# Selective-scan kernel: the last state of each group gets its input from another PSUM bank, and VectorE's passes stand in other steps

## The chip, the cores and the metric

The kernel runs on one core of one Trainium2 chip. The metric is the device time of one execution in microseconds (us), as the median of several runs; smaller is better. The kernel before takes 1560.38 us (three runs, 1560.03 to 1560.77).

## The reference, cut to what matters

x has 8 sequences of 1024 tokens with 256 features, float32. A Mamba layer with a residual is followed by a feed-forward layer with a residual; both begin with a layer norm.

```python
xz = x @ in_proj_w.T                 # 256 -> 2 x 512: xp and z
xc = silu(causal_conv4(xp))
dt, B, C = split(xc @ x_proj_w.T)    # 64, 16, 16
delta = softplus(dt @ dt_proj_w.T + dt_proj_b)
h[t] = exp(delta[t] * A) * h[t-1] + delta[t] * B[t] * xc[t]     # 512 channels x 16 states
y[t] = sum over states of h[t] * C[t] + D * xc[t]
x = x + (y * silu(z)) @ out_proj_w.T
x = x + shared_ffn(layernorm(x)) + routed_ffn(...)
```

The routed experts' weights are truncated to whole numbers; they are almost always zero, and then that part is skipped.

## The kernel before

Work goes by chunks of 512 tokens: 16 chunks c, two to a sequence (HV = 2). Channels lie on the partitions, in 4 groups g of 128. A chunk has S = 32 steps s, eight to a group; a step handles Q = 2 of the 16 states of its group over all 512 tokens. k = 32c + s counts steps. Each engine has its queue written out by hand, step by step (`tensor`, L446; `scalar`, L805; `vector`, L1116; `gpsimd`, L1326; `sync`); semaphores tie them together. TensorE's queue runs two steps behind VectorE's for the sums.

In a step:
- ScalarE writes da = exp(delta * A) for step k + 5 (`act_exp`, L638).
- VectorE scans both states (`dve_scan`, L974): h = da * h + B*u, where B*u is read from BX, four PSUM banks that hold four states of one group. u is delta * xc.
- GpSimd multiplies hs by C (`pool_times_c`, L1271).
- TensorE adds the products of step k - 2 to Y by eight transposes (`pe_sum`, L263), and at the end of each odd step refills BX with B*u of the next four states (`pe_bx`, L239): for each of 4 token blocks and 4 row quarters one matmul of uT (u transposed) with bd, a matrix that holds B on block diagonals. There is one BX, so a refill waits until all four states in it are scanned (`e.wait_ge(s_scan, RT * m)`, L228), and the next scan waits for the refill.

Beside this run, spread over the steps, for neighbouring chunks: the input product and convolution (`pe_xp` L299, `act_xp` L673 and L675, three taps on VectorE, L1005 and L1009, in the bank of Y that is idle); delta (`pe_dt` L349, `act_softplus` L741 to L745, `dve_delta` L1044); u (`pool_u` L1289) and its transposes (`pe_ut` L357, `act_ut` L758); dbc and B transposed (L333, L723, L340, L730), from which SP's queue writes bd by DMA (`sp_bd`, L1406); the gate (L1066), transposed (`pe_yt`, L365; `act_yt`, L765); output product, second norm and shared layer (L376, L1072, L1028, L1035, L775, L386, L396, L1082, L404, L413, L1113). x of chunk c + 2 is transposed in two halves (`pe_trc` L273, `act_trc` L654). Banks PA and PB are shared by these in an order written in BANK_A and BANK_B (step: stage, chunk offset, index): each user waits until the one before it has released the bank. VectorE's passes stand behind the scans of odd steps. `pe_fill` (L444) and others put in matmuls with no use for the result in places where TensorE would stand idle.

## Time and profile before

| | |
|---|---|
| median of 3 runs | 1560.38 us |
| profiled execution, span | 1559.1 us |
| TensorE matmuls busy | 1454.6 us, 93% |
| TensorE weight loads busy | 1134.1 us, 73% |
| VectorE busy | 1475.8 us, 95% |
| ScalarE busy | 1257.4 us, 81% |
| GpSimd busy | 1399.0 us, 90% |
| granted TensorE clock, mean | 0.999 |

The span is the time from the first to the last instruction of the profiled execution; it is 1.3 us below the median of the runs. Engines are PE (TensorE matmuls), PEld (its weight loads), DVE (VectorE), ACT (ScalarE), POOL (GpSimd) and SP (SyncE). Lines are those of the kernel before. In a timeline, rows of like instructions are merged: start, length, engine, line, operation, output and input, count, and in brackets the idle time ahead of it and what ended that.

### The profile page before, as it was taken

The page shows a single profiled execution, that of the slowest core. Times are in us where ns is not written, and L with a number is a line of the kernel's source. Part 1 is how long each engine was busy: PE and PEld are TensorE (multiplying, and loading weights), DVE is VectorE, ACT ScalarE, POOL GpSimd, SP SyncE. Part 2 cuts the span into 40 slices and gives each one's busy share as a digit, 9 for nine tenths or more (in the row PEclk, how much of TensorE's full clock was granted, in tenths as well). Part 3 has the DMA queues.
Part 4 walks back from the last instruction along what each step waited for, and adds up shares of the span by engine and source line. Part 5 has one row for each costly group of instructions (what it writes and reads, how often), then busy time and mean ns, then how long its engine had stood idle before and what let it go on. Part 6 is the DMA issues. An engine that isn't in the chain of part 4 may idle for free.

```text
span 1559.1 us, 39641 instructions
## 1 busy us (share of the span) xinstructions
PE 1454.6 (93%) x15324; PEld 1134.1 (73%) x15324; DVE 1475.8 (95%) x1775; ACT 1257.4 (81%) x2099; POOL 1399.0 (90%) x1199
## 2 busy tenths in 40 slices
PE   8889999999999999999999999999999999999988
PEld 5666777776777777777777777767777677777777
DVE  6999999999999999999999999999999999998886
ACT  7987887887888888887887888888888887788752
POOL 2899999999999999998999989999998999989994
PEclk9999999999999999999999999999999999999999
DMA  5103031040402305032040301304031040401301
GB/s 161 61 3 136 2 101 66 9 157 3 143 22 65 101 3 164 1 93 73 4 163 3 138 28 47 120 3 164 2 97 69 4 149 3 137 15 43 123 2 56
DMA packets 78512, 106.48 MB, mean 68 GB/s; under 512 B 42289, under 2 KB 67761, under 8 KB 70130
## 3 DMA queue, kind: packets, MB, share of 16 engines
q1 hardware_dynamic: 78322, 103.92, 20.8%
q8 instruction: 123, 2.02, 0.5%
q14 instruction: 67, 0.55, 0.1%
HBM read 86.10 MB, written 17.30 MB: 66 GB/s over the span
## 4 chain that ended last, share of the span: by engine, by line
DVE 32%; PE 20%; ACT 18%; issue 17%; POOL 10%; DMA 1%; SPq 1%; DVEq 1%; ACTq 0%; POOLq 0%
DVE hs L974 29%; PE BX L239 9%; ACT da L638 8%; POOL hs L1271 8%; PE Y L299 3%; PE Y L263 2%; ACT xc L705 1%; DMA cb<-c_scratch 1%; SPq L1406 1%; ACT xp L673 1%; DVE st L986 1%; DVE Y L1005 1%; PE PB L349 1%; ACT x2n L775 1%; POOL rstd L1304 1%
## 5 line engine op out<-in xcount | busy, mean ns | idle before, releaser
L1271 POOL TENSOR_TENSOR hs<-hs,cb 128x1024 f32<-128x1024 f32 x512 | 1210.2, 2364 | 76.3 <-DVE hs L974 55.3
L974 DVE TENSOR_TENSOR_SCAN hs<-da,BX 128x512 f32<-128x512 f32 x1024 | 1165.6, 1201 | 55.5 <-PE BX L239 46.5
L638 ACT ACTIVATE da<-delta,a_neg 128x511 f32<-128x511 f32 (+1 forms) x1024 | 663.6, 711 | 24.9 <-DVE hs L974 24.5
L263 PEld LDWEIGHTS Y<-ident,hs 128*128 128x128 f32 x4096 | 464.5, 141 | 97.3 <-issue 58.0
L263 PE MATMUL Y<-ident,hs 128*128 128x128 f32 x4096 | 510.1, 273 | 14.5 <-POOL hs L1271 14.4
L239 PE MATMUL BX<-bd,uT 32*128 32x128 f32 x8192 | 301.3, 284 | 77.9 <-DVE hs L974 73.8
L239 PEld LDWEIGHTS BX<-bd,uT 32*128 32x128 f32 x8192 | 252.5, 187 | 138.8 <-DVE hs L974 137.7
L299 PE MATMUL Y<-xnT,w_in 128*128 128x512 f32 x240 | 117.6, 613 | 0.7 <-ACT gate L691 0.7
L673 ACT ACTIVATE xp<-Y 128x512 f32<-128x512 f32 x60 | 35.9, 598 | 100.4 <-PE Y L299 99.9
L324 PE MATMUL PA<-w_in,xnT 128*128 128x512 f32 x240 | 114.5, 599 | 0.0
L1005 DVE SCALAR_TENSOR_TENSOR Y<-xp,w_conv,Y 128x512 f32<-128x512 f32 x120 | 88.9, 741 | 3.0 <-ACT Y L675 1.4
L1289 POOL TENSOR_TENSOR u<-delta,xc 128x512 f32<-128x512 f32 x63 | 80.4, 1277 | 5.1 <-issue 5.1
L1267 POOL COPY hlast<-hs 128x2 f32<-128x2 f32 x256 | 47.7, 186 | 38.5 <-DVE hs L974 36.8
L324 PEld LDWEIGHTS PA<-w_in,xnT 128*128 128x128 f32 x240 | 43.2, 190 | 44.9 <-issue 43.1
L741 ACT ACTIVATE u<-PB 128x512 f32<-128x512 f32 x63 | 37.5, 596 | 46.8 <-PE PB L349 45.1
L349 PE MATMUL PB<-dbc,w_dt 97*128 97x512 f32 x126 | 70.9, 645 | 0.9 <-DVE dbc L1136 0.9
L758 ACT ACTIVATE uT<-PB 128x512 f32<-128x512 f32 x48 | 28.7, 597 | 49.8 <-PE PB L357 49.8
L299 PEld LDWEIGHTS Y<-xnT,w_in 128*128 128x128 f32 x240 | 40.8, 190 | 36.5 <-issue 28.7
L333 PE MATMUL PA<-xc,w_x 128*96 128x512 f32 x128 | 61.6, 603 | 0.2 <-ACT xc L687 0.2
L376 PE MATMUL PB<-w_out,ygT 128*128 128x256 f32 x240 | 60.8, 386 | 0.9
L376 PE MATMUL PA<-w_out,ygT 128*128 128x256 f32 x240 | 60.8, 386 | 0.0
L1281 POOL TENSOR_TENSOR da<-first,hlast 128x2 f32<-128x2 f32 x256 | 51.1, 199 | 0.0
(194 smaller groups left out, 1517.5 us busy)
## 6 DMA issues: line engine op xcount, KB each, us to landing
cb<-c_scratch SPq DMA_DIRECT2D x64, 1024.0 KB, 4.8
x<-in_x SPq DMA_DIRECT2D x16, 512.0 KB, 4.3
x_scratch<-x2T SPq DMA_DIRECT2D x16, 512.0 KB, 6.8
xt<-in_x SPq DMA_DIRECT2D x15, 512.0 KB, 5.3
bd<-bt SPq DMA_DIRECT2D x480, 1.0 KB
out<-x SPq DMA_DIRECT2D x15, 512.0 KB, 3.2
w_in<-in_in_wT SPq DMA_DIRECT2D x1, 1024.0 KB, 8.4
c_scratch<-dbc SPq DMA_DIRECT2D x64, 8.0 KB, 1.5
```

Of the source, the lines that this page charges most:

```text
L239: mm = e.matmul(BX[:, q * CH + j * P:q * CH + (j + 1) * P], uT[rows, g, j, :], bd[rows, (NR * c + p) % BR, j, :, :].rearrange("p t n -> p ...
L263: mm = e.matmul(Y[(G * c + g) % 2][:, t * P:(t + 1) * P], hs[:, k % HR, q, t * P:(t + 1) * P], ident[:, :], is_transpose=True, start=False ...
L299: mm = e.matmul(bank[:, :], w_in[:, kk, g * P:(g + 1) * P], xnT[c % 2][:, kk, :], start=(kk == 0), stop=(kk == KD - 1))
L324: mm = e.matmul(bank[:, :], xnT[c % 2][:, kk, t * P:(t + 1) * P], w_in[:, kk, ED:2 * ED], start=(kk == 0), stop=(kk == KD - 1))
L333: mm = e.matmul(PA[0:FX, :], w_x[:, g, :], xc[:, (G * c + g) % XR, :], start=(g == 0), stop=(g == G - 1))
L349: e.matmul(bank[:, :], w_dt[:, g * P:(g + 1) * P], dbc[:, :].rearrange("f (j q t) -> f q j t", j=J, q=RT), start=True, stop=True).then_inc ...
L376: mm = e.matmul(bank[:, t2 * DM:(t2 + 1) * DM], ygT[:, g, t * P:(t + 1) * P], w_out[:, g, :], start=(g == 0), stop=(g == G - 1))
L638: e.activation(da[:, k % DR, q, h:], delta[:, g, h:], ACT.Exp, scale=a_neg[:, g, n:n + 1]).then_inc(s_da, 1)
L974: e.tensor_tensor_scan(hs[:, k % HR, q, :], da[:, k % DR, q, :], BX[:, :].rearrange("p (t n) -> p n t", n=RT)[:, n % RT, :], float(c % HV) ...
L1005: e.scalar_tensor_tensor(out=bank[:, :], in0=xp[:, g, kk:kk + CH], scalar=w_conv[:, g, kk:kk + 1], in1=bank[:, :], op0=ALU.mult, op1=ALU.a ...
L1271: e.tensor_tensor(hs[:, k % HR, :, :], hs[:, k % HR, :, :], cb[:, Q * p:Q * p + Q, :], ALU.mult).then_inc(s_hc, 1)
L1289: e.tensor_tensor(u[:, m % UR, :].rearrange("p (j q t) -> p q j t", j=J, q=RT), delta[:, g, :].rearrange("p (q j t) -> p q j t", j=J, q=RT ...
```

## The change

State 15 of each group is no longer computed into BX. ScalarE multiplies uT by B's column of state 15 (`act_v`, four instructions, in steps 5, 13, 20 and 29), and TensorE transposes the result (`pe_bu`, four transposes, in steps 7, 15, 23 and 31) into a bank of its own: the bank of Y that is idle for groups 0, 1 and 3, PA for group 2. The second scan of a group's last step reads that bank. The refill behind such a step waits for 15 states of the group instead of 16, and the refill of the last four states of a group writes three of them. B transposed (`bt`) has two buffers. VectorE's scans of a step are separate calls, with passes between and behind them in other steps than before; two of the other users of PA and PB move to Y[0] (the first half of the shared product, z of block 1), and delta and u of group 1, uT of group 1, the transposes of the gate and of x stand in other steps. Fill matmuls go from steps 7 and 23 to 25. `prob` shares its memory with `is_top`. Of the schedule of VectorE the new lines are shown; renamed variables are left out.

```diff
-          12: [("trc0", 2, 0)], 16: [("z", 1, 1)], 18: [("dbc", 1, 0)], 22: [("bt", 1, 0)],
+          12: [("trc0", 2, 0)], 18: [("dbc", 1, 0)], 22: [("bt", 1, 0)], 23: [("bu", 0, 2)],
           24: [("otr", -1, 0)], 25: [("otr", -1, 1)], 27: [("hl", -1, 1)], 30: [("z", 1, 2)]}
...
+BANK_B = {2: [("yt", -1, 2), ("trc", 2, 0)], 3: [("trc", 2, 1)], 4: [("ut", 0, 1)], 6: [("dt", 0, 2)],
+          8: [("res", -1, 0)], 13: [("trc0", 2, 1)], 16: [("dt", 0, 3)], 18: [("yt", 0, 0)], 20: [("ut", 0, 3)],
+          21: [("yt", 0, 1)], 24: [("dt", 1, 0)], 26: [("hl", -1, 0)], 28: [("ut", 1, 0)], 29: [("ht", -1, 0)],
+          30: [("dt", 1, 1), ("yt9", 0, 2)]}
...
-        bt = sb("bt", [P, NR, J, RT])
+        bt = [sb(f"bt{i}", [P, NR, J, RT]) for i in range(2)]
+        v = sb("v", [P, J, P])
...
-        prob = sb("prob", [P, NQ, TB, NE])
+        prob = is_top
...
+            if (stage, i) == ("o", 0):
+                return Y[0], c, s_o0, s_o0_out
+            if (stage, i) == ("z", 1):
+                return Y[0], c - 1, s_z1, s_z1_out
+            if stage == "bu" and i != 2:
+                return Y[(i + 1) % 2], 3 * c + min(i, 2), s_bu, s_bu_out
...
+        def scanned(k):
+
+            c, i = divmod(k, S)
+            g, p = divmod(i, NP)
+            return released("bu", c, g) if p == NP - 1 else (s_scan, (N - 1) * (G * c + g) + Q * (p + 1))
+
...
         def pe_bx(e, m):
             c, i = divmod(m, QC)
             g, p = divmod(i, NR)
-            e.wait_ge(s_scan, RT * m)
+            e.wait_ge(s_scan, (N - 1) * (m // NR) + RT * p)
...
+            ns = RT - 1 if p == NR - 1 else RT
             for j in range(J):
                 for q in range(RT):
                     rows = slice(q * KT, (q + 1) * KT)
-                    mm = e.matmul(BX[:, q * CH + j * P:q * CH + (j + 1) * P], uT[rows, g, j, :],
-                                  bd[rows, (NR * c + p) % BR, j, :, :].rearrange("p t n -> p (t n)"), start=True,
+                    mm = e.matmul(BX[:, q * CH + j * P:q * CH + (j + 1) * P].rearrange("p (t n) -> p t n", n=RT)[:, :, 0:ns],
+                                  uT[rows, g, j, :], bd[rows, (NR * c + p) % BR, j, :, 0:ns], start=True,
                                   stop=True, tile_position=(q * KT, 0))
             mm.then_inc(s_bx, 1)
+
+        def pe_bu(e, c, g):
+            bank, n, done, out = bank_of("bu", c, g)
+            e.wait_ge(out, n)
+            if g != 2:
+                e.wait_ge(s_gm, G * c + g)
+            conv = {0: 5 if c == 0 else G * c + 6, 1: G * c + 7, 3: G * c + 9}.get(g, 0)
+            if conv and on(c + 1 if g < 2 else c + 2):
+                e.wait_ge(s_yx_out, conv - G + 1)
+            e.wait_ge(s_v, G * c + g + 1)
+            for j in range(J):
+                mm = e.transpose(bank[:, :].rearrange("p (q j t) -> p j q t", q=RT, j=J)[:, j, :, :], v[:, j, :], ident[:, :])
+            mm.then_inc(done, 1)
         def pe_skip(e, c, g):
             m = G * c + g
             e.wait_ge(s_gm, max(0, m - 1))
+            if m:
+                e.wait_ge(*released("bu", *divmod(m - 1, G)))
+            if g == 2 and on(c + 1):
+                e.wait_ge(*released("z", c + 1, 1))
+            if g == 0 and on(c - 2):
+                e.wait_ge(*released("o", c - 2, 0))
...
+            if v == G + 2:
+                e.wait_ge(*released("bu", 0, 0))
...
         def pe_z(e, c, t):
             bank, n, done, out = bank_of("z", c, t)
             e.wait_ge(out, n)
+            if t == 1:
+                e.wait_ge(*released("bu", c - 1, 1))
...
         def pe_shared(e, c, kk):
             bank, n, done, out = bank_of("o", c, kk)
             e.wait_ge(out, n)
+            if kk == 0:
+                e.wait_ge(*released("bu", c + 1, G - 1))
...
+            e.wait_ge(*released("bu", *divmod(m - 1, G)))
...
-                    if s == 2:
+                    if s == 4:
...
-                    if s == 2 and c and on(c + 2):
-                        pe_trc(e, c + 2, 0)
                     if s in (12, 13) and c == 0:
                         pe_trc(e, 2, s - 12)
                     if on(c - 1):
+                        if s == 2:
+                            pe_yt(e, c - 1, 2)
                         if s == 4:
-                            pe_yt(e, c - 1, 2)
...
+                    if s % NP == NP - 1:
+                        pe_bu(e, c, s // NP)
...
-                    if s == 3 and c and on(c + 2):
-                        pe_trc(e, c + 2, 1)
-                    if s == 15:
+                    if s in (2, 3) and c and on(c + 2):
+                        pe_trc(e, c + 2, s - 2)
+                    if s == 18:
...
-                    if c == NQ - 2 and s in (23, 29):
+                    if c == NQ - 2 and s in (25, 29):
                         pe_fill(e, c, s, 5)
-                    if c == NQ - 1 and s in (5, 7, 13, 17, 21, 23, 29):
+                    if c == NQ - 1 and s in (5, 13, 17, 21, 25, 29):
...
+            e.wait_ge(*released("bu", NQ - 1, G - 1))
...
         def act_exp(e, k, parts=range(2)):
             c, i = divmod(k, S)
             g, p = divmod(i, NP)
-            e.wait_ge(s_scan, max(0, Q * (k - DR + 1)))
+            if k >= DR:
+                e.wait_ge(*scanned(k - DR))
...
 +        def act_v(e, c, g):
+            m = G * c + g
+            e.wait_ge(*released("ut", c, g))
+            if c:
+                e.wait_ge(*released("bt", c, 0))
+            else:
+                e.wait_ge(s_b15, 1)
+            if m:
+                e.wait_ge(*written("bu", *divmod(m - 1, G)))
+            for j in range(J):
+                ins = e.activation(v[:, j, :], uT[:, g, j, :], ACT.Copy, scale=bt[c % 2][:, NR - 1, j, RT - 1:RT])
+            ins.then_inc(s_v, 1)
...
         def act_bt(e, c):
             bank, n, done, out = bank_of("bt", c, 0)
             e.wait_ge(done, n + 1)
-            e.wait_ge(s_bdd, 16 * KT * (c - 1))
-            e.activation(bt[:, :, :, :], bank[:, 0:J * FX].rearrange("p (j f) -> p j f", j=J)[:, :, R:R + N].rearrange(
+            e.wait_ge(s_bdd, 16 * KT * max(0, c - 2))
+            e.activation(bt[c % 2][:, :, :, :], bank[:, 0:J * FX].rearrange("p (j f) -> p j f", j=J)[:, :, R:R + N].rearrange(
                 "p j (r n) -> p r j n", r=NR), ACT.Copy).then_inc(out, 1)
 ...
-                    if s == 2:
-                        act_ut(e, c, 1)
+                    if s == 2 and on(c - 1):
+                        act_yt(e, c - 1, 2)
                     if s in (3, 4) and c and on(c + 2):
                         act_trc(e, c + 2, s - 3)
                     if s == 4 and c and on(c + 1):
                         act_xp(e, G * c + 6)
                     if s == 4 and on(c - 1):
-                        act_yt(e, c - 1, 2)
                         act_yt(e, c - 1, 3)
+                    if s == 4:
+                        act_ut(e, c, 1)
...
-                    if s == 8:
-                        act_silu_z(e, c)
+                    if s in (5, 13, 20, 29):
+                        act_v(e, c, s // NP)
                     if s in (12, 13) and c == 0:
                         act_trc(e, 2, s - 12)
                     if s == 7:
                         if on(c + 1):
                             act_z(e, c + 1, 0)
                         act_skip(e, c, 1)
+                    if s == 8:
+                        act_silu_z(e, c)
                     if s == 5 and c == 0:
                         act_norm(e, 2)
                     if s == 15:
                         act_skip(e, c, 2)
+                    if s == 18:
...
-        def dve_scan(e, k):
+        def dve_scan(e, k, q):
             c, i = divmod(k, S)
             g, p = divmod(i, NP)
-            e.wait_ge(s_bx, k // 2 + 1)
-            e.wait_ge(s_y, max(0, k - HR + 1))
-            if c % HV:
-                e.wait_ge(s_cr, S * (c // HV) + i + 1)
-            for q in range(Q):
-                n = Q * p + q
-                e.wait_ge(s_da, Q * k + q + 1)
+            if q == 0:
+                e.wait_ge(s_bx, k // 2 + 1)
+                e.wait_ge(s_y, max(0, k - HR + 1))
+                if c % HV:
+                    e.wait_ge(s_cr, S * (c // HV) + i + 1)
+            n = Q * p + q
+            e.wait_ge(s_da, Q * k + q + 1)
+            if n == N - 1:
+                bank, use, done, out = bank_of("bu", c, g)
+                e.wait_ge(done, use + 1)
+                e.tensor_tensor_scan(hs[:, k % HR, q, :], da[:, k % DR, q, :], bank[:, :],
+                                     float(c % HV), ALU.mult, ALU.add).then_inc(out, 1)
+            else:
...
         def dve_bd(e, p):
             if p == 0:
                 e.wait_ge(*written("bt", 0, 0))
+            if p == NR - 1:
+                e.tensor_copy(bt[0][:, NR - 1, :, RT - 1], PA[:, 0:J * FX].rearrange("p (j f) -> p j f", j=J)[
+                    :, :, R + N - 1]).then_inc(s_b15, 1)
...
+                e.wait_ge(s_b15, 1)
...
+                    dve_scan(e, k, 0)
+                    if s == 14 and on(c + 1):
+                        dve_tap(e, G * c + 7 if c else G + 3, 1)
+                    if s == 24 and on(c + 2):
+                        dve_tap(e, G * c + 8, 0)
+                    dve_scan(e, k, 1)
+                    if s == 1:
+                        if c == 0:
+                            dve_tap(e, G, 0)
+                            dve_tap(e, G, 1)
+                        else:
+                            if on(c - 2):
+                                dve_shared(e, c - 2, 0)
+                            dve_delta(e, c, 1)
+                    if s == 3:
+                        if c == 0:
+                            dve_tap(e, G, 2)
+                        if on(c - 2):
+                            dve_shared(e, c - 2, 1)
+                        if on(c - 1):
+                            dve_gate(e, c - 1, 3)
+                    if s == 5 and on(c + 1):
+                        dve_tap(e, G * c + 6 if c else G + 1, 0)
+                        dve_tap(e, G * c + 6 if c else G + 1, 1)
+                    if s == 6 and on(c + 1):
+                        dve_tap(e, G * c + 6 if c else G + 1, 2)
                     if s == 7:
                         dve_delta(e, c, 2)
+                    if s == 9:
+                        if c == 0:
+                            for kk in range(K - 1):
+                                dve_tap(e, G + 2, kk)
+                        elif on(c + 3):
                             dve_stats(e, c + 3, 0)
                             dve_stats(e, c + 3, 1)
+                    if s == 11:
+                        dve_gate(e, c, 0)
+                        if on(c - 1):
+                            dve_residual(e, c - 1, 0)
+                    if s == 13:
+                        if on(c + 1):
+                            dve_tap(e, G * c + 7 if c else G + 3, 0)
+                        if on(c - 1):
+                            dve_stats2(e, c - 1, 0)
+                    if s == 14 and on(c + 1):
+                        dve_tap(e, G * c + 7 if c else G + 3, 2)
+                    if s == 17:
+                        if on(c - 1):
+                            dve_residual(e, c - 1, 1)
+                        dve_delta(e, c, 3)
+                    if s == 19:
+                        dve_gate(e, c, 1)
+                        if on(c - 1):
+                            dve_stats2(e, c - 1, 1)
+                    if s == 21:
+                        if on(c - 1):
+                            dve_aggr2(e, c - 1)
+                        if on(c + 3):
                             dve_aggr(e, c + 3)
+                    if s == 24 and on(c + 2):
+                        dve_tap(e, G * c + 8, 1)
+                    if s == 25:
+                        if on(c + 2):
+                            dve_tap(e, G * c + 8, 2)
+                        if on(c + 1):
                             dve_delta(e, c + 1, 0)
+                    if s == 27:
+                        dve_gate(e, c, 2)
+                        if on(c - 1):
+                            dve_top(e, c - 1, 0)
+                    if s == 28 and on(c - 1):
+                        dve_top(e, c - 1, 1)
+                    if s == 29 and on(c + 2):
+                        dve_tap(e, G * c + 9, 0)
+                        dve_tap(e, G * c + 9, 1)
+                    if s == 30 and on(c + 2):
+                        dve_tap(e, G * c + 9, 2)
...
         def pool_times_c(e, k):
             c, i = divmod(k, S)
             g, p = divmod(i, NP)
-            e.wait_ge(s_scan, Q * (k + 1))
+            e.wait_ge(*scanned(k))
...
-            e.wait_ge(s_scan, Q * (k - DR + 1))
+            e.wait_ge(*scanned(k - DR))
...
+                        if s == 1 and c:
+                            pool_u(e, c, 1)
                         if s == 7:
                             pool_u(e, c, 2)
                         if s == 17:
                             pool_u(e, c, 3)
-                    if on(c + 1):
-                        if s == 25:
-                            pool_u(e, c + 1, 0)
-                        if s == 31:
-                            pool_u(e, c + 1, 1)
+                    if s == 25 and on(c + 1):
+                        pool_u(e, c + 1, 0)
...
-                            bt[t:P:KT, :, :, :]).then_inc(s_bdd, 16)
+                            bt[c % 2][t:P:KT, :, :, :]).then_inc(s_bdd, 16)
```

## Rows read from the trace of the kernel before

**Rows 1.** The page: busy us, share of the span, instructions of each engine
```profile
PE 1454.6 (93%) x15324; PEld 1134.1 (73%) x15324; DVE 1475.8 (95%) x1775; ACT 1257.4 (81%) x2099; POOL 1399.0 (90%) x1199
```

**Rows 2.** Windows: us; busy (count) of PE, PEld, DVE, ACT, POOL; granted clock; DMA share; GB/s
```profile
694.00:788.00 94.00, 89.20 (x946) 69.35 (x945) 91.79 (x111) 78.87 (x134) 87.31 (x71) 1.00 0.23 71
...
1501.30:1504.70 3.40, 3.40 (x40) 3.17 (x41) 2.55 (x5) 0.47 (x1) 2.95 (x4) 0.50 0.00 0
```

**Rows 3.** Waits of VectorE: total us, times, longest us
```profile
DVE hs L974 <- PE BX L239: 46.5, 76, 1.3
```

**Rows 4.** Timeline of VectorE in chunk 7 (its step 5 ends at 709.8)
```profile
709.78 1.52 DVE L1005 SCALAR_TENSOR_TENSOR Y<-xp,w_conv,Y 128x512 f32<-128x512 f32 x2
711.21 4.55 DVE L974 TENSOR_TENSOR_SCAN hs<-da,BX 128x512 f32<-128x512 f32 x4
715.68 0.72 DVE L1009 SCALAR_TENSOR_TENSOR xc<-xp,w_conv,Y 128x512 f32<-128x512 f32 x1
716.32 0.68 DVE L1044 SCALAR_TENSOR_TENSOR delta<-PB,u 128x512 f32<-128x512 f32 x1
717.06 4.55 DVE L974 TENSOR_TENSOR_SCAN hs<-da,BX 128x512 f32<-128x512 f32 x4
...
745.55 0.74 DVE L1028 BATCH_NORM_STATS2 st<-x 128x6 f32<-128x256 f32 x2
...
758.04 4.56 DVE L974 TENSOR_TENSOR_SCAN hs<-da,BX 128x512 f32<-128x512 f32 x4 [0.76 <-PE BX L239]
...
774.84 0.24 DVE L1082 MAX8 top<-PB 128x8 f32<-128x8 f32 x2
775.11 0.17 DVE L1084 TENSOR_TENSOR is_top<-PB,top 128x16 f32<-128x16 f32 x1
```

**Rows 5.** Timeline of TensorE's matmuls in chunk 7 (steps 2, 5 to 7, 21 to 23)
```profile
700.39 1.03 PE L413 MATMUL PA<-w_s,x2n 128*128 128x256 f32 x4
701.25 0.60 PE L273 MATMUL PB<-ident,xt 128*128 128x128 f32 x4
...
709.92 1.17 PE L239 MATMUL BX<-bd,uT 32*128 32x128 f32 x32
711.02 1.12 PE L349 MATMUL PB<-dbc,w_dt 97*128 97x512 f32 x2
711.99 1.04 PE L263 MATMUL Y<-ident,hs 128*128 128x128 f32 x8
712.86 1.88 PE L324 MATMUL PA<-w_in,xnT 128*128 128x512 f32 x4
...
715.81 0.39 PE L239 MATMUL BX<-bd,uT 32*128 32x128 f32 x4 [0.20 <-DVE hs L974]
...
757.91 1.99 PE L299 MATMUL Y<-xnT,w_in 128*128 128x512 f32 x4
759.73 0.49 PE L340 MATMUL PA<-ident,dbc 96*128 96x96 f32 x4
760.06 1.91 PE L263 MATMUL Y<-ident,hs 128*128 128x128 f32 x16
762.65 0.39 PE L239 MATMUL BX<-bd,uT 32*128 32x128 f32 x4 [0.68 <-DVE hs L974]
```

**Rows 6.** Groups by shape: count, busy us, mean ns of one, idle before
```profile
L752 ACT ACTIVATE xc<-xc,d_skip 128x512 f32<-128x512 f32 x64 | 45.4, 710 | 0.0
L730 ACT ACTIVATE bt<-PA 128x64 f32<-128x64 f32 x15 | 3.3, 223 | 16.2 <-PE PA L340 16.2
```

**Rows 7.** Timeline of ScalarE in chunk 7, steps 2 and 3
```profile
700.64 1.32 ACT L638 ACTIVATE da<-delta,a_neg 128x511 f32<-128x511 f32 x2
701.89 0.60 ACT L654 ACTIVATE xnT<-PB 128x512 f32<-128x512 f32 x1
```

**Rows 8.** Timeline of VectorE behind the last scan
```profile
1537.87 2.31 DVE L1093 SCALAR_TENSOR_TENSOR prob<-den,is_top 128x480 f32<-128x480 f32 x1 [0.29 <-ACT den L792]
```

**Rows 9.** Timeline of TensorE in chunk 15
```profile
1501.16 1.14 PE L239 MATMUL BX<-bd,uT 32*128 32x128 f32 x16 [2.06 <-DVE hs L974]
```

83 lines of the change are left out of this document (11 added, 72 removed).

## The prediction

> **What bounds the kernel now.** I read the page's busy times first: VectorE 95%, TensorE's matmuls 93%, GpSimd 90% [rows 1]. No engine has much air, so the question is which order of events repeats. The windows show a chunk of 94 us at the full granted clock, with TensorE busy for 89.2 us of it and VectorE for 91.8 us [rows 2]. VectorE waits for the refill of BX 76 times, 46.5 us in all [rows 3]; those are only the waits that a profile can see.
>
> The timeline of VectorE shows the rhythm [rows 4]. Four scans take 4.55 us: each is 1.20 us long and the next starts 1.11 us after it. Then BX, of which there is one copy, has to be refilled. The scans that began at 711.21 end at 715.76; at 715.81 the refill starts on TensorE and takes 1.17 us [rows 5], and the next scan starts at 717.06: 1.30 us from the last scan's end, though the passes between (715.68, 716.32) are done before. Two taps in a gap run 1.52 us and stretch it by 0.05 us (709.78 to 711.21). From the start of one refill to the next it is therefore 5.85 us, in three of sixteen cases 5.90. A chunk is 13 x 5.85 + 3 x 5.90 = 93.75 us, and sixteen chunks make 1500 of the 1559.1 us. The kernel is bound by "four scans, then a refill"; passes in the gap cost nothing up to 1.3 us.
>
> The timeline of TensorE shows how late the next refill could be without anybody noticing [rows 5]. Consecutive groups overlap by 0.16 us, so a group costs its length less 0.16; behind BX, 1.10; and a refill that follows without idle time costs 0.09 more. Steps 6 and 7 hold 1.10 + 0.97 + 0.87 + 1.72 + 0.87 + 0.09 = 5.62 us against 5.89 granted: only 0.2 to 0.3 us of air. VectorE's floor and TensorE's floor lie that close in many pairs of steps.
>
> **The change, part by part.** I time refill starts, naming each by the step behind which it comes (R5 to R7 and so on).
>
> *State 15 leaves BX.* The refill behind steps 7, 15, 23 and 31 may start after the third scan, and the fourth, 1.11 us, lies in the gap. That takes 4 x 1.11 = 4.4 us a chunk off VectorE's path if the refill really starts then.
>
> *Passes leave the gaps.* Six taps and one pair of top-8 passes now run between scans that no refill separates. A tap costs 0.64 us there (715.68 to 716.32 [rows 4]), the top-8 passes about 0.40 (two maxima and the comparison, 774.84 to 775.11 and 0.17 less overlap). In a gap they cost nothing before; now they cost 6 x 0.64 + 0.40 = 4.2 us a chunk. This alone eats what state 15 saved.
>
> *The refill of a group's last four states writes three of four columns.* It was 1.17 us for 32 matmul records of 128 columns. The row with 96 columns (four transposes of dbc, 0.49 us against 0.60 for 128 columns [rows 5]) says that time goes with columns: bounds 0.96 (all scales) and 1.17 (nothing does). I take 0.97, 0.20 less, as the nearest row scales.
> The Trainium skill (TensorE: Matmul & The Clock Gate, section "Wait — 56ns, not 53.3ns?") speaks against that: starts of matmuls are never closer than about 25 ns. BX's are 29 ns apart here; by the rule the refill would shrink by 0.12 us only, and the sum below would be some 4 us higher. No row shows it.
>
> *TensorE's four transposes (bu)* cost 0.60 - 0.16 = 0.44 us, and stand in its queue ahead of a sum (0.87) and of the refill. In steps 7, 15 and 31 they wait for the last tap of the convolution that uses the same bank, and everything behind them waits too.
>
> *ScalarE's four scalings* of 128 columns: the nearest rows are 0.22 us (64 columns) and 0.71 (512 columns) [rows 6]; four cost 0.9 to 2.8, I take 1.3. ScalarE is busy for 78.9 of 94 us [rows 2] and writes da about five steps ahead, so they lie in idle time. The upper bound would delay delta in step 7 by some 0.3 us (low bound: nothing).
>
> *GpSimd and SP's queue* keep their work; u of group 1 moves from step 31 to step 1 and is ready before its transposes in step 4. The copies for bd read a second buffer and are issued no later. B is scaled out of its own copy. The copy added before the first chunk lies where VectorE has 0.5 us idle. Merging prob with is_top costs nothing.
>
> Now the sixteen intervals of an inner chunk. VectorE's path: refill 1.24 to the first scan (1.04 with three columns), 1.11 a scan, 1.20 for the last, 0.05 to the next refill.
> - R5 to R7: VectorE 1.29 + 2.22 + 0.64 + 1.20 + 0.05 = 5.40; TensorE 0.90 (1.10 less 0.20) + 0.97 + 0.87 + 1.72 + bu 0.44 + 0.87 + 0.09 = 5.87. TensorE decides: -0.03 against 5.90. R29 to R31 has the same instructions: +0.02.
> - R13 to R15: scans and taps reach the end of the last tap 4.76 us after R13: a tap and two statistics (745.55 [rows 4]) fill 1.18, then 1.11 + 0.64 + 1.11 + 0.72; then bu, sum and refill: + 0.05 + 0.44 + 0.87 + 0.09 = 6.22. +0.32.
> - R21 to R23: VectorE could at 4.51. TensorE 0.90 + 1.82 + 0.33 + 1.75 + 0.44 + 0.09 = 5.33 [rows 5]: -0.52.
> - R23 to R25: two taps between the scans: 1.24 + 3 x 1.11 + 1.28 + 1.20 + 0.05 = 7.10: +1.20.
> - R27 to R29: the second top-8 passes: +0.40.
> - R1 to R3: both transposes of x now have one sum between them instead of two. The second needs ScalarE's copy of the first out of the same bank, and that stands behind yT's copy and two exps (1.32 [rows 7]). Refill, skip, shared product and yT's transposes end 3.06 us after R1 (1.10 + 0.49 + 0.87 + 0.60 [rows 5]); then 0.53 + 1.22 + 0.60 on ScalarE, and 0.6 us of transposes: refill 0.16 us late. The second copy holds uT's bank: 0.04 more in R3 to R5.
> - The other eight stay at 5.85. In the gaps of steps 21, 23, 27 and 31 VectorE idles as before or more (0.76 us at 758.04 was there already [rows 4]).
>
> Sum: -0.03 + 0.02 + 0.32 - 0.52 + 1.20 + 0.40 + 0.16 + 0.04 = +1.6 us a chunk, 13 inner chunks: +20.7. Chunk 0, with less on TensorE, about +0.8; chunk 14 +0.8; the last has no taps and little on TensorE, two of its groups save about 1 us each and the top-8 passes cost 0.4: -1.4. Tail: the product that goes into Y[0] waits for the last scan, and the 2.31 us pass at 1537.87 [rows 8] with it: +0.8. Total +21.7 on an execution with a span of 1559.1, 1.3 under the median of 1560.4: **1582 us**.
>
> **Rivals.**
> *TensorE keeps up (faster).* If refill and transposes were always ready when VectorE comes, R5 to R7 is 5.40 but R7 to R9 6.15 (state 15 and delta fill 1.6 us), R13 to R15 5.93, R21 to R23 4.51, R29 to R31 5.40, R1 to R5 unchanged: 93.4 us a chunk, with the ends 1555 us. For it: BX has 0.2 to 0.7 us of air before most refills (0.68 at step 23). Against it: the air is smaller than what bu and the earlier start ask, by 0.8 us in step 23. It decides where a pair's matmuls take less than VectorE's 4.5 to 5.4 us.
> *They cancel:* half of TensorE's lateness, no wait for the tap: about 1560.
> *The short refill is no shorter and the scalings are dear:* R5 to R7, R21 to R23 and R29 to R31 each 0.2 longer, 0.15 for delta: some 10 us, 1592.
> *The clock falls.* In the last chunk TensorE once stood idle for 2.06 us [rows 9] and a stretch of 3.4 us at 0.50 of the clock (1.2 GHz) followed [rows 2], which made that interval 0.8 us longer. R23 to R25 now has about 2.4 us of idle time on TensorE in two pieces; if the clock fell there in each chunk: +11 us, 1594. Elsewhere idle pieces of 1 us left the clock at 1.00, so I think it unlikely.
>
> **How the numbers follow.** A measurement of this kernel tells about 0.2%, 3 us, from no change. The forecast, about +1% to +2%, gets 0.62; refill not shorter or the clock 0.18; cancelling 0.07; TensorE keeps up 0.13. Faster 0.13, same 0.07, slower 0.80. The range goes from the faster rival, 1555, to a little over the dear cases, 1600; the slower cases alone fill 1566 to 1600.
>
> **What would show it.** In the changed profile: the refill behind step 23 starts some 0.8 us after its third scan instead of 0.05; between R23 and R25 7.1 us; a wait of VectorE for BX behind state 15 in steps 15, 23 and 31 (0.3 to 0.9 us) and still 0.6 in step 21; a refill record of about 0.97 us behind steps 5, 13, 21, 29; chunks of 95.4 us. Chunks under 93.7 us would refute the argument, above all if TensorE's refill starts on time behind state 14.

## The result, and the profile after

The changed kernel takes 1614.16 us (median of four runs, 1612.09 to 1615.67), the kernel before in the same session 1560.3 us (1560.03 to 1560.77). The ratio is 1.0343, with an interval of 1.0328 to 1.0357: 3.4% slower. The forecast was 1582 us in a range of 1555 to 1600; the direction was right and the size less than half of what came. All times below are medians of runs like these; one run of all, of "State 15 back in BX", took 2091.56 us at a mean granted clock of 0.65, and it is left out.

The page's busy times of the kernel after:

```profile
PE 1487.4 (92%) x15568; PEld 1162.1 (72%) x15568; DVE 1479.0 (92%) x1776; ACT 1328.7 (82%) x2355; POOL 1403.0 (87%) x1199
```

Beside [rows 1], VectorE has 3 us more work and 55 us more of span: its loss is waiting. ScalarE has 71 us more, which is a first hint. The chain of waits shows it by pairs (who waits, for whom, us, how often, mean us), in the kernel after:

```profile
DVE hs L1043 <- PE BX L256: 89.8, 122, 2.8
PEld PA L416 <- ACT uT L817: 15.1, 15, 1.2
PE Y L271 <- DVE xc L1078: 19.4, 15, 2.9
```

VectorE's waits for BX have nearly doubled against [rows 3] (46.5 us, 76 times). The other two are new, and each comes about once a chunk: TensorE waits for ScalarE's copy of uT, and the new transposes (L271) wait for the last tap. To place them I took the start of the first scan behind each refill from the trace. Mean of chunks 1 to 13, us, "R5 to R7" being the stretch from the refill behind step 5 to the one behind step 7 (differences are taken before rounding):

| stretch | before | forecast difference | after | difference |
|---|---|---|---|---|
| R1 to R3 | 5.85 | +0.16 | 6.08 | +0.23 |
| R5 to R7 | 5.84 | -0.03 | 6.00 | +0.16 |
| **R9 to R11** | 5.85 | **0** | 6.70 | **+0.85** |
| R11 to R15 | 11.74 | +0.32 | 12.38 | +0.64 |
| R19 to R25 | 17.67 | +0.68 | 18.52 | +0.85 |
| R25 to R29 | 11.70 | +0.40 | 12.26 | +0.56 |
| R29 to R31 | 5.85 | +0.02 | 5.98 | +0.13 |
| the other five | 29.30 | +0.04 | 29.31 | +0.01 |
| chunk | 93.80 | +1.6 | 97.24 | +3.44 |

The prediction timed the starts of the refills themselves. By these, R5 to R7 is 6.04, R13 to R15 6.54, R21 to R23 5.51 and R29 to R31 6.03 us, where 5.87, 6.22, 5.33 and 5.87 were forecast; the chunk is the same.

13 x 3.44 = 44.7 us. Chunk 0 costs 3.50 more, chunk 14 2.94, the last 1.45 less; the start is 0.77 and the tail 4.24 longer. The sum, 54.7, is the difference of the spans (1613.8 less 1559.1). Half of the chunk's extra is in two places, and one of them was not forecast at all.

**R9 to R11, where nothing was forecast.** TensorE's timeline in steps 10 and 11 of chunk 7, after (start, length, engine, line, operation, count, idle time ahead and what ended it):

```profile
747.81 0.60 PE L397 MATMUL PA<-ident,u 128*128 128x128 f32 x4
749.11 1.04 PE L299 MATMUL Y<-ident,hs 128*128 128x128 f32 x8
751.07 1.13 PE L416 MATMUL PA<-w_out,ygT 128*128 128x256 f32 x4 [0.92 <-ACT uT L817]
```

The transposes of u are written into PA at 747.81 and the output product wants PA at 750.15; it gets it at 751.07, when ScalarE has copied uT out. ScalarE's timeline over the same time, after:

```profile
736.82 1.27 ACT L764 ACTIVATE v<-uT,bt 128x128 f32<-128x128 f32 x4
...
744.68 1.28 ACT L773 ACT_TABLE_LOAD   x1
745.97 1.91 ACT L773 ACTIVATE gate<-gate 128x2048 f32<-128x2048 f32 x1
747.90 1.28 ACT L774 ACT_TABLE_LOAD   x1
749.20 1.33 ACT L684 ACTIVATE da<-delta,a_neg 128x511 f32<-128x511 f32 x2
750.44 0.57 ACT L817 ACTIVATE uT<-PA 128x512 f32<-128x512 f32 x1
```

The copy (750.44) is the last of a row without a gap: the gate's SiLU, between two table loads of 1.28 us, then two exps. The four scalings at 736.82 have pushed this whole row back by their length.

**R21 to R25, where most was forecast.** TensorE's timeline in steps 22 and 23 of chunk 7, after, and VectorE's in steps 22 to 24:

```profile
786.16 1.04 PE L299 MATMUL Y<-ident,hs 128*128 128x128 f32 x8
787.04 0.60 PE L271 MATMUL PA<-ident,v 128*128 128x128 f32 x4
787.48 1.04 PE L299 MATMUL Y<-ident,hs 128*128 128x128 f32 x8
788.44 1.17 PE L256 MATMUL BX<-bd,uT 32*128 32x128 f32 x32
```

```profile
785.28 2.31 DVE L1043 TENSOR_TENSOR_SCAN hs<-da,BX 128x512 f32<-128x512 f32 x2
787.75 1.22 DVE L1040 TENSOR_TENSOR_SCAN hs<-da,PA 128x512 f32<-128x512 f32 x1 [0.15 <-PE PA L271]
789.68 1.22 DVE L1043 TENSOR_TENSOR_SCAN hs<-da,BX 128x512 f32<-128x512 f32 x1 [0.72 <-PE BX L256]
790.82 0.73 DVE L1074 SCALAR_TENSOR_TENSOR Y<-xp,w_conv,Y 128x512 f32<-128x512 f32 x1
791.46 1.21 DVE L1043 TENSOR_TENSOR_SCAN hs<-da,BX 128x512 f32<-128x512 f32 x1
792.59 0.73 DVE L1074 SCALAR_TENSOR_TENSOR Y<-xp,w_conv,Y 128x512 f32<-128x512 f32 x1
```

BX is free at 787.59, TensorE is without any idle time and comes to the refill at 788.44, 0.85 us later (0.8 in the prediction). Scan and TensorE's transposes lie beside each other as meant, but VectorE then waits 0.72 us, and in the next pair the two taps between scans are on its path for their whole length. R23 to R25 is 7.17 us (7.10 forecast).

**R13 to R15.** TensorE's timeline, after:

```profile
758.85 1.15 PE L256 MATMUL BX<-bd,uT 32*128 32x96 f32 x32 [0.15 <-DVE hs L1043]
...
761.76 1.04 PE L299 MATMUL Y<-ident,hs 128*128 128x128 f32 x8
763.95 0.63 PE L271 MATMUL Y<-ident,v 128*128 128x128 f32 x4 [1.16 <-DVE xc L1078]
764.42 1.04 PE L299 MATMUL Y<-ident,hs 128*128 128x128 f32 x8
```

A refill of three states takes 1.15 us, one of four 1.17: it is hardly shorter. And the bank of Y is free only behind the third tap of the convolution (it ends at 763.69), 0.26 us before the transposes start; sum and refill stand behind them in TensorE's queue.

**The ends.** In chunk 0 and in the tail TensorE stands idle and then runs at half the clock. Its rows at the starts of the two stretches, and the windows of those (busy us of PE, PEld, DVE, ACT and POOL, granted clock, DMA share, GB/s), after:

```profile
82.93 1.08 PE L271 MATMUL Y<-ident,v 128*128 128x128 f32 x4 [2.93 <-DVE xc L1078]
1587.65 1.73 PE L463 MATMUL Y<-w_s,x2n 128*128 128x256 f32 x4 [2.00 <-DVE hs L1040]
```

```profile
82.90:86.20 3.30, 3.27 (x23) 2.97 (x27) 2.12 (x2) 1.23 (x3) 2.53 (x3) 0.51 0.00 0
1588.00:1591.40 3.40, 3.40 (x10) 2.69 (x9) 1.91 (x3) 0.30 (x2) 2.16 (x1) 0.50 0.02 5
```

At 82.93 four transposes take 1.08 us instead of 0.60. The granted clock is 0.5 (1.2 GHz) in both; R13 to R15 of chunk 0 alone is 2.2 us longer. The wait and the lower clock can be told apart in the tail. The runs with four columns and with the scalings in step 3 (below) have the same queue there and the same wait of 2.00 us, but the clock stays at 1.00, and from the first scan behind the last refill to the end they take 29.18 and 29.19 us. The kernel after and three other runs with this queue, all at the lower clock, take 30.87 to 30.89. Of the 4.24 us the clock is therefore 1.7. The run with four columns:

```profile
1589.02 1.10 PE L463 MATMUL Y<-w_s,x2n 128*128 128x256 f32 x4 [2.00 <-DVE hs L1040]
```

**Chunk 13.** The clock fell in one inner chunk too, behind a wait of 1.88 us for the refill of step 25. In chunk 11 TensorE has as much idle time between R23 and R25, 2.08 us, but in two pieces of 0.84 and 1.24 us. TensorE's row in chunk 13, and the window behind it, after:

```profile
1378.66 1.17 PE L256 MATMUL BX<-bd,uT 32*128 32x128 f32 x32 [1.88 <-DVE hs L1043]
```

```profile
1379.80:1383.20 3.40, 3.40 (x20) 3.40 (x17) 3.35 (x4) 1.39 (x4) 3.40 (x4) 0.50 0.08 9
```

R25 to R27 of that chunk is 6.94 us for 5.85. This one place is the whole +0.08 of R25 to R27 in the mean.

### The profile page after: what moved, and what is told of

It reads as the page before. It is cut to its first block, busy times and chain, and to the rows that moved or that the text cites. A ratio compares the mean times of both kernels' runs of the same rounds, so it can differ in the third digit from the quotient of the medians.

```text
span 1613.8 us, 40703 instructions
## 1 busy us (share of the span) xinstructions
PE 1487.4 (92%) x15568; PEld 1162.1 (72%) x15568; DVE 1479.0 (92%) x1776; ACT 1328.7 (82%) x2355; POOL 1403.0 (87%) x1199
## 4 chain that ended last, share of the span: by engine, by line
PE 29%; DVE 26%; issue 19%; ACT 17%; POOL 5%; DMA 2%; SPq 1%; DVEq 1%; ACTq 0%; POOLq 0%
DVE hs L1043 22%; PE BX L256 12%; ACT da L684 7%; PE Y L299 5%; POOL hs L1354 4%; PE Y L337 3%; DVE Y L1074 3%; PE PA L364 1%; ACT v L764 1%; SPq L1488 1%; ACT L774 1%; ACT L773 1%; DMA cb<-c_scratch 1%; PE PA L416 1%; PE Y L271 1%
## 5 line engine op out<-in xcount | busy, mean ns | idle before, releaser
L1043 DVE TENSOR_TENSOR_SCAN hs<-da,BX 128x512 f32<-128x512 f32 x960 | 1105.1, 1203 | 97.0 <-PE BX L256 89.8
L299 PE MATMUL Y<-ident,hs 128*128 128x128 f32 x4096 | 523.5, 273 | 17.2 <-POOL hs L1354 16.3
L364 PE MATMUL PA<-w_in,xnT 128*128 128x512 f32 x180 | 86.2, 601 | 0.0
L764 ACT ACTIVATE v<-uT,bt 128x128 f32<-128x128 f32 x256 | 81.2, 392 | 0.0
L1040 DVE TENSOR_TENSOR_SCAN hs<-da,Y 128x512 f32<-128x512 f32 x48 | 58.2, 1212 | 1.3 <-ACT da L684 0.7
L824 ACT ACTIVATE ygT<-PB 128x512 f32<-128x512 f32 x48 | 28.1, 586 | 34.8 <-PE PB L405 34.8
```

Source lines behind the costliest of these rows:

```text
L299: mm = e.matmul(Y[(G * c + g) % 2][:, t * P:(t + 1) * P], hs[:, k % HR, q, t * P:(t + 1) * P], ident[:, :], is_transpose=True, start=False ...
L364: mm = e.matmul(bank[:, :], xnT[c % 2][:, kk, t * P:(t + 1) * P], w_in[:, kk, ED:2 * ED], start=(kk == 0), stop=(kk == KD - 1))
L764: ins = e.activation(v[:, j, :], uT[:, g, j, :], ACT.Copy, scale=bt[c % 2][:, NR - 1, j, RT - 1:RT])
L1043: e.tensor_tensor_scan(hs[:, k % HR, q, :], da[:, k % DR, q, :], BX[:, :].rearrange("p (t n) -> p n t", n=RT)[:, n % RT, :], float(c % HV) ...
```

## The experiments

Each starts from the changed kernel and differs by the edit shown, with the last three excepted: they build on one another, from the run with all repairs on. Of the run with state 15 back in BX and of the one with all repairs the main lines are shown. A difference is counted against the changed kernel, the ratio against the kernel before on the same chip (medians 1560.3 to 1560.9 us).

**State 15 back in BX, the passes left where the change put them.** It removes the scalings, the transposes and the early refill.

```diff
-            return released("bu", c, g) if p == NP - 1 else (s_scan, (N - 1) * (G * c + g) + Q * (p + 1))
+            return s_scan, Q * (k + 1)
...
-            e.wait_ge(s_scan, (N - 1) * (m // NR) + RT * p)
+            e.wait_ge(s_scan, RT * m)
...
-                        pe_bu(e, c, s // NP)
...
-                        act_v(e, c, s // NP)
```

> State 15 is computed into BX and scanned from there as before the change; ScalarE's scalings and TensorE's transposes for it are left out; everything else of the change, above all where VectorE's passes stand, is kept. This is the price of the new places of the passes alone. Theory A: passes between scans cost their full length: R5 to R7 6.49, R13 to R15 7.13, R23 to R25 7.13, R27 to R29 6.25, R29 to R31 6.54 us, the rest 5.85 and 5.90: 98.0 us a chunk against 93.8, so about 1560 + 15 x 4.2 = 1620 to 1625, a little above the changed kernel: the idle bank then saves under 1 us a chunk of the 4.4 it takes out of the scans. Rival B: the passes cost little and the transposes and scalings are what made it slow: between 1560 and 1590.

1641.28 us (median of three runs), 1.0520 (1.0499 to 1.0542), 16 us above the upper end of what was expected. R9 to R11 has lost its extra (5.85 us). The chunk is 5.25 us longer than before, but that mean is of two kinds of chunk: 98.28 us (98.0 were expected from the passes alone), and 99.75 in every second one, where the clock falls. TensorE's row in chunk 7, the window behind it, and the same row one chunk later, in this kernel:

```profile
777.67 1.93 PE L256 MATMUL BX<-bd,uT 32*128 32x128 f32 x32 [2.32 <-DVE hs L1036]
```

```profile
777.00:782.00 5.00, 4.33 (x36) 2.85 (x37) 2.97 (x4) 0.44 (x1) 2.84 (x4) 0.66 0.00 0
```

```profile
877.42 1.17 PE L256 MATMUL BX<-bd,uT 32*128 32x128 f32 x32 [2.32 <-DVE hs L1036]
```

The wait is 2.32 us in both, in steps 14 and 15; behind the first TensorE is at the lower level and its refill takes 1.93 us, behind the second it is not. So theory A holds: a pass between scans costs its length. And the idle bank is worth something: with it the mean chunk is 1.8 us shorter than with these passes alone, some 1.0 of it at the full clock and 0.8 because the clock falls less often. It has to pay for the passes, 4.5 us at the full clock, and does not.

**Refill with all four columns.**

```diff
-            ns = RT - 1 if p == NR - 1 else RT
+            ns = RT
```

> The refill of a group's last four states writes all four columns again (128 columns a matmul instead of 96). Theory A: with 96 columns it takes as long as with 128 (1.15 to 1.17 us in the changed kernel's profile), because something other than the columns sets the pace, so nothing changes: 1614, within 3 us. Rival B, the one in my prediction: 0.20 us are saved somewhere in each of four refills, three of which decide; then the time rises by 14 x 0.6 = 8 us.

1614.82 us, 1.0343 (1.0326 to 1.0360): no difference beyond the noise. The 0.20 us that the prediction took off each three-column refill are 0.03 in the trace (1.15 us for 1.17).

**Refill with one column**, to see whether columns matter at all. States 13 and 14 are then not refilled.

```diff
-            ns = RT - 1 if p == NR - 1 else RT
+            ns = 1 if p == NR - 1 else RT
```

> The refill of a group's last four states writes one of four columns (32 a matmul); states 13 and 14 are scanned from what was in the bank. It asks what sets the refill's 1.17 us. Theory A: something that does not go with the columns (the 32 weight loads, or a smallest distance between matmuls): 1.1 to 1.17 us again, matmuls 28 to 29 ns apart. Rival B: a smallest distance of about 25 ns: 0.78 + 0.27 = 1.05 us. Rival C: columns: 0.5 us. The time changes by under 3 us in A.

One run: 1614.27 us. The refill takes 1.10 us with 32 columns instead of 1.15 with 96. Its beginning, cut off behind the first 4 and behind the first 16 of the 32 records, in the kernel after (96 columns) and then in this one (32):

```profile
734.33 0.36 PE L256 MATMUL BX<-bd,uT 32*128 32x96 f32 x4
734.33 0.70 PE L256 MATMUL BX<-bd,uT 32*128 32x96 f32 x16
```

```profile
733.70 0.32 PE L256 MATMUL BX<-bd,uT 32*128 32x32 f32 x4
733.70 0.65 PE L256 MATMUL BX<-bd,uT 32*128 32x32 f32 x16
```

The first four differ by 0.04 us; the next twelve add 0.34 and 0.33 us. By the single starts in the trace the records come in eight packs of four: the four of a pack start 7 ns apart, and from the second pack on a pack starts 112 ns behind the one before, with 128, 96 and 32 columns alike. Only the first distance goes with the columns (213, 187 and 133 ns). So theory A has the size (1.10 us, and the time did not change), but its 28 to 29 ns, as rival B's 25, would be a mean of 7 and 92 (26.5 here): what costs is one of eight packs. What sets the 112 ns is not shown; the weight loads of the packs start 108 to 112 ns apart as well, and no run changed them. The chunk follows the refill: 97.31 us with four columns, 97.24 with three, 97.10 with one.

**The scalings in step 3.**

```diff
-                    if s in (5, 13, 20, 29):
+                    if s in (3, 13, 20, 29):
                         act_v(e, c, s // NP)
```

> One part of the changed kernel is moved: ScalarE's four scalings for group 0 stand in step 3, where ScalarE waits 2.5 us for the convolution's input anyway, instead of step 5. Theory A: the interval of steps 10 and 11 is 6.70 us instead of 5.85 because the scalings (1.27 us) push the SiLU of z with its two table loads, and behind it the copy of uT of group 2, 1 us back, and TensorE's output product waits for that copy to leave bank PA. Then this interval falls back to 5.85 to 5.95 us and the time falls by 14 x 0.8 = 11 to 12 us, to about 1602. Rival B: the interval is long because TensorE has too much to do in it; then nothing changes (1614, within 3 us).

1613.16 us, 1.0336 (1.0319 to 1.0354), where 1602 was expected. R9 to R11 is back at 5.85 us: the scalings were the cause. But R3 to R5 grew by 0.84, and the time stayed. TensorE there, in this kernel:

```profile
728.94 1.17 PE L256 MATMUL BX<-bd,uT 32*128 32x128 f32 x32
...
731.35 0.66 PE L397 MATMUL PB<-ident,u 128*128 128x128 f32 x4 [1.24 <-ACT xnT L700]
```

Now the copy of xnT out of PB is late, and the transposes of u wait for it. The miss moved to the next user of a bank.

**The scalings in step 4**, ahead of the input product's copy.

```diff
+                    if s == 4:
+                        act_v(e, c, 0)
...
-                    if s in (5, 13, 20, 29):
+                    if s in (13, 20, 29):
```

> As the run with the scalings of group 0 in step 3, but behind the copy of x's second half in step 4, ahead of the convolution's input for which ScalarE waits 2.5 us. In step 3 the long interval of steps 10 and 11 went (6.70 to 5.85) but steps 4 and 5 grew by 0.84, since that copy holds bank PB for uT. Theory A (ScalarE's order, no lack of time): both intervals are at 5.85 to 5.90 now, 14 x 0.85 = 12 us less, about 1602. Rival B (ScalarE has no 1.2 us to give in this part of the chunk): one of the intervals of steps 4 to 11 is again 0.5 us or more too long, and the time stays above 1608.

1603.70 us, 1.0270 (1.0253 to 1.0287). R9 to R11 is 5.85 and R3 to R5 5.90, as before; the chunk is 2.59 longer instead of 3.44. The same work one step earlier costs nothing: it was ScalarE's order, not a lack of time. The output product has no wait here:

```profile
745.48 1.07 PE L416 MATMUL PA<-w_out,ygT 128*128 128x256 f32 x4
```

**The new transposes behind the sum instead of ahead of it.**

```diff
-                    if s % NP == NP - 1:
-                        pe_bu(e, c, s // NP)
...
                         pe_sum(e, k - 2)
+                    if s % NP == NP - 1:
+                        pe_bu(e, c, s // NP)
```

> The four transposes of the scaled state stand behind the sum of the same step instead of ahead of it. Theory A: in steps 14 and 15 TensorE stands idle for 1.2 us, waiting for the last tap in the bank that it wants to write, with a sum behind it that could run; with the sum ahead, that refill comes 0.87 us earlier (interval 6.56 to 5.75 or 5.95, the bound of the scans and two taps), and the others, where TensorE is not idle, stay: 15 x 0.65 = 9 to 10 us less, about 1604. Rival B: TensorE's queue is full there too and only the order changes: no change; or state 15, scanned later, holds up VectorE in steps 7, 23 and 31: slower by up to 0.4 us a place, up to 15 us.

1607.90 us, 1.0300 (1.0283 to 1.0318), where theory A expected 1604. R13 to R15 (+0.72 in the changed kernel; R11 to R13 gives 0.08 back) falls to +0.21, R9 to R11 from +0.85 to +0.14, while R5 to R7 rises from +0.16 to +0.83. TensorE's row in step 15, its row in step 7 and VectorE's in step 7, of this kernel:

```profile
760.66 0.63 PE L271 MATMUL Y<-ident,v 128*128 128x128 f32 x4 [0.28 <-DVE xc L1078]
```

```profile
736.54 0.60 PE L271 MATMUL Y<-ident,v 128*128 128x128 f32 x4
```

```profile
735.20 1.21 DVE L1043 TENSOR_TENSOR_SCAN hs<-da,BX 128x512 f32<-128x512 f32 x1
737.25 1.22 DVE L1040 TENSOR_TENSOR_SCAN hs<-da,Y 128x512 f32<-128x512 f32 x1 [0.83 <-ACT da L684]
```

The wait for the tap is shorter when the sum stands ahead of it (0.28 us for 1.16). In step 7 the opposite: the scan of state 15 stands 0.83 us for its bank. The row names da, which was written long ago; of several waits the trace names one, and TensorE's transposes end at 737.14, 0.11 us before the scan starts. The gain in R9 to R11 is the other side of that loss: VectorE and TensorE come later, ScalarE does not, and the output product waits 0.20 us for the copy of uT instead of 0.92. From R5 to R11 the sum is the same (+1.02 and +1.04); what the run gains stands in R13 to R15. So the place is right for group 1, and for group 0 it costs what R9 to R11 gives back.

**Both taps of step 24 in the gap behind step 23.**

```diff
-                    if s == 24 and on(c + 2):
-                        dve_tap(e, G * c + 8, 0)
...
-                    if s == 24 and on(c + 2):
+                    if s == 23 and on(c + 2):
+                        dve_tap(e, G * c + 8, 0)
```

> One pair of taps goes back: the first two taps of the convolution's group 0, which the change put between the scans of step 24, stand behind the scans of step 23 again, in the gap of a refill. (Group 2's state 15 uses bank PA, so nothing forbids it.) Theory A: a pass between scans costs its length, in the gap of step 23 almost nothing, since TensorE's refill is late there anyway: the interval of steps 24 and 25 falls from 7.17 to 5.9 us, that of 22 and 23 stays at 5.54 to 5.7: 14 x 1.1 to 1.2 us less, about 1598. Rival B: TensorE, not VectorE, needs those 7.17 us (its products wait for GpSimd), then at most 0.4 us a chunk, 1608 or more.

1602.78 us, 1.0270 (1.0253 to 1.0288), where theory A expected 1598. VectorE, in this kernel:

```profile
782.63 1.22 DVE L1040 TENSOR_TENSOR_SCAN hs<-da,PA 128x512 f32<-128x512 f32 x1 [0.16 <-PE PA L271]
783.77 1.52 DVE L1074 SCALAR_TENSOR_TENSOR Y<-xp,w_conv,Y 128x512 f32<-128x512 f32 x2
785.20 4.55 DVE L1043 TENSOR_TENSOR_SCAN hs<-da,BX 128x512 f32<-128x512 f32 x4
```

The taps (1.52 us) fill the 0.72 us wait for BX and stick out on both sides: R21 to R23 goes from 5.54 to 6.17, R23 to R25 from 7.17 to 5.84 us. Together -0.70, some 10 us over the kernel: two taps cost 1.3 us between scans and 0.6 us in this gap, where state 15 and a wait of 0.72 us already are; at most 0.16 was expected.

**All repairs together**: scalings in step 4, transposes of group 1 behind the sum, the taps in the gap of step 23, the top-8 passes of step 28 back in a gap, in the tail the output products of the first token block ahead of the product that waits for the last scan, and ScalarE's copy of the first half of xnT in step 2 instead of 3 (the second stays in step 4).

```diff
-                    if s in (3, 4) and c and on(c + 2):
-                        act_trc(e, c + 2, s - 3)
+                    if s in (2, 4) and c and on(c + 2):
+                        act_trc(e, c + 2, s // 2 - 1)
```

> All repairs together: scalings of group 0 in step 4, transposes of group 1 behind the sum, the pair of taps in the gap of step 23, both top-8 passes in step 27, ScalarE's copy of x's first half ahead of an exp, and output products ahead of the last wait for VectorE. If each measured or computed loss stands by itself: of the 3.44 us a chunk, 0.85 + 0.5 + 1.15 + 0.45 + 0.2 go, 0.3 stay; 1560 + 13 x 0.3 + 3 or so: about 1568 (1562 to 1576), level with the kernel before or a little slower, because TensorE's lateness behind steps 7, 23 and 31 remains. If the idea itself were what is slow (Rival: more work for TensorE and ScalarE with no air), it would stay above 1585.

1582.62 us, 1.0143 (1.0126 to 1.0160), 14.6 us above what was expected. 11 of them are R3 to R5 (6.74 for 5.90 us, 13 times): four exps, in two steps, now lie between the two copies. The scalings (R9 to R11 5.85 us), the transposes (R13 to R15 6.06), the top-8 passes (R27 to R29 5.90) and the first copy (R1 to R3 5.85) gave what was computed, the taps 0.70 us a chunk for 1.15. In the tail TensorE no longer waits for the last scan; the tail takes 26.98 us for 30.87, 0.35 more than before.

**The same with the copies in steps 2 and 3.**

```diff
-                    if s in (2, 4) and c and on(c + 2):
-                        act_trc(e, c + 2, s // 2 - 1)
+                    if s in (2, 3) and c and on(c + 2):
+                        act_trc(e, c + 2, s - 2)
```

> The run with all repairs, but ScalarE copies both halves of x's transposes a step earlier, in steps 2 and 3 (there: 2 and 4). In that run the interval of steps 2 and 3 fell by 0.24 to 5.85, but steps 4 and 5 grew by 0.84 to 6.74: two pairs of exps stood between the copies, and the second copy holds bank PB, which uT of group 1 wants. Theory A: with one pair between them both intervals are at 5.85 to 5.90 and 94.5 us a chunk are left: 13 x 0.84 = 11 us less than 1582.6, about 1571. Rival B: ScalarE falls behind elsewhere (its exps come later) and the 0.84 us turn up in another interval: above 1578.

1571.89 us, 1.0075 (1.0058 to 1.0092), as expected (1571). The chunk is 94.46 us. What is left stands in R5 to R7 (6.00), R13 to R15 (6.05), R21 to R23 (6.16) and R29 to R31 (5.98): the four that hold the new transposes.

This kernel and the run with all repairs have the same program in chunk 0, and it shows the price of the clock there. TensorE's transposes of step 15, in the run with all repairs and in this one:

```profile
82.38 0.63 PE L271 MATMUL Y<-ident,v 128*128 128x128 f32 x4 [0.96 <-DVE xc L1082]
```

```profile
82.19 1.09 PE L271 MATMUL Y<-ident,v 128*128 128x128 f32 x4 [0.97 <-DVE xc L1082]
```

Behind the same wait the clock is 1.00 in the first and 0.50 in the second, and R13 to R15 of this chunk takes 6.06 and 7.06 us; in the changed kernel, with 2.93 us of wait and the lower clock, it took 8.06.

**One of the four new transposes.** State 15 of the other three token blocks is scanned from what the bank held.

```diff
-            for j in range(J):
+            for j in range(1):
```

> As the run with both copies early, but of the four transposes of the scaled state one is done; state 15 of the other three token blocks is scanned from what was in the bank. 0.33 us of TensorE's work go from the queue ahead of each of four refills. Theory A, TensorE's own time sets what is left over the kernel before (steps 6 and 7 5.99 to 6.07, 22 and 23 6.16, 30 and 31 5.98 us): the intervals of 6 and 7 and of 30 and 31 fall by 0.2 to 0.33, that of 14 and 15 by at most 0.1 (two taps and scans bind it), that of 22 and 23 by up to 0.1 (state 15 and two taps fill its gap): 13 x 0.5 = 6 to 8 us less, 1564 or so. Rival B: the wait of state 15 for its bank or VectorE's passes bind there; then under 2 us.

1560.74 us, 1.0000 (0.9990 to 1.0009): 11 us less than the run before, where theory A expected 6 to 8 (R21 to R23 fell by 0.26 us, not by at most 0.1). TensorE in step 7 of chunk 7, of the kernel before this edit and with it:

```profile
720.43 0.60 PE L271 MATMUL Y<-ident,v 128*128 128x128 f32 x4
720.87 1.04 PE L299 MATMUL Y<-ident,hs 128*128 128x128 f32 x8
721.83 1.17 PE L256 MATMUL BX<-bd,uT 32*128 32x128 f32 x32
```

```profile
716.27 0.27 PE L271 MATMUL Y<-ident,v 128*128 128x128 f32 x1
716.38 1.04 PE L299 MATMUL Y<-ident,hs 128*128 128x128 f32 x8
717.35 1.17 PE L256 MATMUL BX<-bd,uT 32*128 32x128 f32 x32
```

Both rows run without idle time, so 0.33 us less of transposes is 0.3 us less of the stretch (R5 to R7 5.71 for 6.00, R29 to R31 5.66 for 5.98). Once ScalarE's order and VectorE's passes are mended, TensorE's own work is what remains of the loss. And even with a quarter of the transposes, the scheme only reaches the kernel before. No version that computes all of it beats that kernel.

## Why the prediction was wrong, point by point

- **"BX bounds, and the air is small on both engines": right.** R5 to R7, R21 to R23 and R29 to R31 went by TensorE, R23 to R25 by VectorE, as written. The refill behind step 23 starts 0.85 us late (0.8 forecast), and R23 to R25 is 7.17 us (7.10).
- **"They lie in idle time" (ScalarE's scalings): the step that failed most, 0.85 of the missing 1.84 us a chunk.** Their size was right (1.27 us for 1.3). But the argument went by ScalarE's busy share and by da, which is five steps ahead. ScalarE's queue also holds the copies out of PA and PB, and those are not ahead: a bank passes from user to user through them. Moved one step, the scalings cost nothing. [rows 7] show such a copy behind exps; the prediction applied that to R1 to R5 alone.
- **"I take 0.97" (the three-column refill): wrong.** It takes 1.15 us, 1.10 even with 32 columns. The row it was scaled from, four transposes with 96 columns, does go with columns; a refill comes in packs of four matmuls, and their distance, 112 ns, does not. By the refills' starts that is +0.17, +0.18 and +0.16 in R5 to R7, R21 to R23 and R29 to R31 against the sum, 0.51 of the missing 1.84. The Trainium skill (TensorE: Matmul & The Clock Gate, section "Wait — 56ns, not 53.3ns?") has starts no closer than about 25 ns. The trace does not agree for these matmuls on 32-row tiles: the four of a pack start 7 ns apart. The prediction's "29 ns apart" is a mean over the packs, so its 0.12 us of shrinking had no ground either (0.03 came). But the rival that it stood for, a refill hardly shorter, was right and belonged into the sum.
- **R13 to R15, +0.32 forecast, +0.64 by the refills' starts.** The chain of terms was right. Mis-sized was above all the way from the tap's end to the transposes, 0.26 us and not 0.05; the tap ended 4.84 us behind the refill's start and not 4.76, and the rest took 0.03 more. With the sum ahead of the transposes, +0.21 remains (by the first scans, where the changed kernel has +0.72).
- **"Chunk 0 +0.8, tail +0.8": wrong**, 3.50 and 4.24. TensorE was thought to have less to do there and so air. It had none to do for 2.93 and 2.00 us, and the clock fell as well. In the tail the mechanism was named (the product into Y[0] waits for the last scan) and mis-sized: 2.6 us at the full clock, and 1.7 for the clock on top. The rival on the clock put its fall into R23 to R25 of each chunk; it came there once in 13 chunks and cost 1.1 us. That it came in this run in chunk 13 and behind the last scan, and in others of the same queue did not, is luck either way.
- **R25 to R29 and R1 to R3**: +0.56 for 0.40, of which 0.08 is the clock in chunk 13, and +0.23 for 0.16: small and of the right kind.

By size, the missing 33 us (54.7 less 21.7) are: 11 for the scalings (0.85 x 13), 7 for the refill's length (0.51 x 13), 4 for R13 to R15 (0.32 x 13), 8.3 for chunk 0, chunk 14 and the tail (10.7 where 2.4 were forecast), 0.8 for the start, which differs from run to run, and 2.1 spread over the rest of the chunks, 1.1 of them the clock in chunk 13.

Three things stay open. Using the idle bank only in the last chunk, where TensorE has air and the changed kernel is 1.45 us faster than the one before, was not tried, and neither was a layout that needs fewer transposes. What sets the 112 ns of a pack was not tested. And in chunk 0 no run parts the wait from the lower clock at the transposes' old place: the two numbers above (6.06 and 7.06 us) are of a kernel that has the sum ahead of them.

## What to carry to other kernels

An engine that is busy 81% of the time has no idle time for new work until its queue has been read instruction by instruction: what counts is which short copy behind the new work releases a bank or buffer to an engine without air. Here two engines were each within 0.3 us of the bound, and work taken off one and put on the other was worth nothing; a pass that lay in a wait must not be moved to where the wait no longer is. Scale the time of a group of short matmuls by columns only if a row of the same kind (the same tiles, as many instructions) shows that columns count, and look at the distances of the single starts before you take their mean for a rule.
